# A two-sided adjacency product: half of the row groups turned in place by ScalarE and VectorE, in two rings of slots

## The chip, the cores and the metric

The kernel runs on one core of a Trainium2 chip. The metric is device time in microseconds (us), lower is better. Inputs and outputs are fp32.

## The reference

`x` is 5120 x 64 and `adj` is 5120 x 5120. Cut to what matters:

```
h = relu(layernorm(x))
e = par[0]*par[1] * (diag[:, None] * h @ W) + h      # users (rows 0:2048) and items have their own W, diag, par
h2 = adj @ (adj.T @ e)
out = x + layernorm(h2) * gamma + beta + h
```

The matrix `adj` (105 MB) is used twice: `adj.T @ e` sums over its rows, and the outer product sums over its columns, for which TensorE needs the tiles of `adj` transposed in SBUF.

## The kernel before

The columns of `adj` are cut into 5 panels of 1024, the rows into 10 groups of 512. One group of one panel is a slot: 128 partitions x 4 x 1024 fp32, 2 MB. Each panel has a **t phase**, in which `sum_t` adds the 10 groups' part of `adj.T @ e` into the PSUM bank `tT_ps`; a **finish**, in which `take_tT` copies the result out, TensorE turns it and `take_t` copies the turned blocks to `t_blocks` (a second set in another row order follows beside the first bank); and an **h phase**, in which `sum_h` adds this panel's part of `adj @ t` into 5 PSUM banks `h_ps`, one for each pair of groups, 8 column blocks of each. The last panel's h phase also has the output layernorm between its banks.

Before the h phase the tiles must be transposed. Three ways are in use, side by side:

- TensorE transposes 3 groups of each panel (4 in the first) in 128 x 128 tiles beside `sum_t` (L730, `turn_tiles`); ScalarE copies them back into the same slot (L430, `slot_back`).
- VectorE transposes 2 groups of each panel in 32 x 32 squares out of the slot into `at_ring`, 16 instructions of 32 x 512 for each half group (L569, `turn_units`); GpSimd copies them back into the slot (L345, `units_back`).
- The other 5 groups (4 in the first panel) are read from HBM a second time in an order in which 32 x 32 squares suffice (L252, `load_second`: two quadrants' DMAs on SP's queue and two on ScalarE's), and VectorE turns them block by block into `at_ring` during the h phase (L615, `turn_second`).

All 10 slots of a panel lie in SBUF (`panel`). The next panel's natural loads (L246, on SP's queue) follow in the order in which `sum_h` lets go of slots. The work is written out by hand for each engine, in order; panels 1 to 3 are a loop. In the first panel the "ego" chain (layernorm of `x`, relu, times W, `e_rows`) runs unit by unit beside the first groups of the t phase, on VectorE, ScalarE, TensorE and GpSimd in turn; TensorE's group 2k of the t phase needs unit k of `e`.

## Time and profile before

| what | value |
|---|---|
| median of 3 runs | 497.58 us (496.18 to 498.24) |
| profiled execution, its own time | 498.96 us |
| its span | 497.2 us |
| TensorE busy | 466.0 us, 94% |
| VectorE busy | 381.5 us, 77% |
| ScalarE busy | 101.0 us, 20% |
| GpSimd busy | 128.6 us, 26% |
| moved by DMA | 158.21 MB |

The span is the stretch of the records; the execution's own time is 1.8 us longer. A busy TensorE is not one at its peak, since the ends of matmuls are modelled; waits are therefore read from the chain of waits, whose pieces are listed in order of time with a start, a length and what ran. A releaser is the instruction whose semaphore ended a wait.

### The profile page before, as it was taken

The page shows a single profiled execution, that of the slowest core. Times are in us where ns is not written, and L with a number is a line of the kernel's source. Part 1 is how long each engine was busy: PE and PEld are TensorE (multiplying, and loading weights), DVE is VectorE, ACT ScalarE, POOL GpSimd, SP SyncE. Part 2 cuts the span into 40 slices and gives each one's busy share as a digit, 9 for nine tenths or more (in the row PEclk, how much of TensorE's full clock was granted, in tenths as well). Part 3 has the DMA queues.
Part 4 walks back from the last instruction along what each step waited for, and adds up shares of the span by engine and source line. Part 5 has one row for each costly group of instructions (what it writes and reads, how often), then busy time and mean ns, then how long its engine had stood idle before and what let it go on. Part 6 is the DMA issues. An engine that isn't in the chain of part 4 may idle for free.

```text
span 497.2 us, 6294 instructions
## 1 busy us (share of the span) xinstructions
PE 466.0 (94%) x2300; PEld 190.3 (38%) x2300; DVE 381.5 (77%) x523; ACT 101.0 (20%) x236; POOL 128.6 (26%) x111
## 2 busy tenths in 40 slices
PE   0799997999999899999999999999899999989996
PEld 0345543333443333244324324533433353344453
DVE  2768996868999735989984598999249899941793
ACT  2134442000340100025001002510200151022222
POOL 1121444180009500000852000075200005640223
PEclk9999999999999989999999999999899999979998
DMA  6999959999994999999599999969999996996001
GB/s 218 393 410 404 354 144 273 297 393 409 410 408 160 331 347 378 409 409 410 195 323 346 377 410 408 411 241 321 347 374 410 408 409 240 281 348 217 22 21 63
DMA packets 82114, 158.21 MB, mean 318 GB/s; under 512 B 4784, under 2 KB 56496, under 8 KB 82096
## 3 DMA queue, kind: packets, MB, share of 16 engines
q1 hardware_dynamic: 54864, 132.72, 72.3%
q10 hardware_dynamic: 27232, 25.26, 17.5%
q8 instruction: 11, 0.18, 0.1%
q14 instruction: 7, 0.06, 0.0%
HBM read 156.65 MB, written 1.31 MB: 318 GB/s over the span
## 4 chain that ended last, share of the span: by engine, by line
PE 69%; DVE 14%; issue 7%; ACTq 4%; DMA 2%; POOL 2%; ACT 1%; DVEq 0%; POOLq 0%
PE tT_ps L748 30%; PE h_ps L813 25%; PE tr_ps L730 10%; DVE at_ring L569 6%; DVE at_ring L615 6%; ACTq L252 3%; DMA diag_sb<-in_L_gnn_diag_i_dram 2%; POOL panel L345 2%; PE tr_ps L786 2%; PE tT_ps L759 1%; PE h_ps L716 1%; DVE e_sb L531 1%; DVE panel L529 0%; PE tT_ps L786 0%; ACT tT_quads L447 0%
## 5 line engine op out<-in xcount | busy, mean ns | idle before, releaser
L569 DVE STREAM_TRANSPOSE at_ring<-panel 32x512 f32<-32x512 f32 x320 | 224.8, 702 | 9.9 <-PE h_ps L813 5.3
L748 PE MATMUL tT_ps<-panel,e_sb 128*64 128x512 f32 x800 | 190.0, 607 | 2.9 <-DVE e_sb L531 2.9
L345 POOL TENSOR_TENSOR panel<-at_ring,ones_sb 128x512 f32<-128x512 f32 x80 | 103.0, 1326 | 288.7 <-PE tT_ps L748 227.7
L615 DVE STREAM_TRANSPOSE at_ring<-panel 128x1024 f32<-128x1024 f32 (+1 forms) x115 | 112.4, 1036 | 29.6 <-PE h_ps L813 21.5
L430 ACT ACTIVATE panel<-tr_ps 128x512 f32<-128x512 f32 x128 | 71.6, 595 | 231.1 <-PE tr_ps L730 230.7
L813 PE MATMUL h_ps<-panel,t_blocks 128*64 128x512 f32 x416 | 109.8, 616 | 0.5 <-POOL panel L345 0.5
L813 PE MATMUL h_ps<-at_ring,t_strided 128*64 128x512 f32 x384 | 100.9, 597 | 0.6
L748 PEld LDWEIGHTS tT_ps<-panel,e_sb 128*64 128x64 f32 x800 | 51.8, 138 | 91.2 <-issue 87.7
L730 PE MATMUL tr_ps<-ident,panel 128*128 128x128 f32 x512 | 76.5, 290 | 9.8 <-ACT tT_sb L446 5.1
L730 PEld LDWEIGHTS tr_ps<-ident,panel 128*128 128x128 f32 x512 | 57.2, 145 | 67.4 <-ACT panel L430 47.1
L813 PEld LDWEIGHTS h_ps<-panel,t_blocks 128*64 128x64 f32 x416 | 33.8, 143 | 67.6 <-issue 65.5
L813 PEld LDWEIGHTS h_ps<-at_ring,t_strided 128*64 128x64 f32 x384 | 30.0, 136 | 50.2 <-issue 28.0
L594 DVE COPY t_strided<-tT_ps 128x512 f32<-128x512 f32 x5 | 3.4, 685 | 26.4 <-PE tT_ps L759 26.4
L446 ACT ACTIVATE tT_sb<-tT_ps 64x512 f32<-64x512 f32 x5 | 3.0, 594 | 93.3 <-issue 51.7
L332 POOL TENSOR_TENSOR x_sb<-x_sb,e_sb 128x512 f32<-128x512 f32 x5 | 6.8, 1359 | 32.9 <-ACT e_sb L415 32.9
L377 POOL TENSOR_TENSOR panel<-panel,gamma_sb 128x512 f32<-128x512 f32 x4 | 5.1, 1273 | 39.3 <-DVE panel L646 39.3
L594 DVE COPY t_blocks<-tT_ps 128x512 f32<-128x512 f32 x5 | 3.5, 692 | 13.3 <-PE tT_ps L759 13.3
L708 PE MATMUL h_ps<-ident,e_sb 128*128 128x128 f32 x20 | 3.6, 309 | 9.9 <-ACT e_sb L415 9.9
L463 ACT ACTIVATE panel<-tr_ps 128x64 f32<-128x64 f32 x32 | 6.6, 239 | 20.3 <-PE tr_ps L786 20.3
L786 PEld LDWEIGHTS tr_ps<-c_blk,panel 128*128 128x128 f32 x36 | 8.8, 326 | 4.8 <-issue 3.2
L786 PE MATMUL tr_ps<-c_blk,panel 128*128 128x128 f32 x36 | 9.7, 411 | 0.7 <-ACT panel L478 0.7
L716 PE MATMUL h_ps<-w_blk,panel 128*128 128x128 f32 x40 | 6.6, 316 | 2.9 <-DMA w_blk<-in_L_gnn_W_i_dram 2.3
(57 smaller groups left out, 108.8 us busy)
## 6 DMA issues: line engine op xcount, KB each, us to landing
panel<-in_adj_dram SPq DMA_DIRECT2D x50, 2048.0 KB, 21.9
panel<-in_adj_dram SPq DMA_DIRECT2D x48, 512.0 KB, 11.5
panel<-in_adj_dram ACTq DMA_DIRECT2D x48, 512.0 KB, 12.7
x_sb<-in_x_dram SPq DMA_DIRECT2D x5, 256.0 KB, 8.7
out_dram<-x_sb SPq DMA_DIRECT2D x10, 128.0 KB, 1.8
w_blk<-in_L_gnn_W_u_dram SPq DMA_DIRECT2D x2, 16.0 KB, 10.1
w_blk<-in_L_gnn_W_i_dram SPq DMA_DIRECT2D x2, 16.0 KB, 9.2
gamma_sb<-in_L_gnn_ln_gamma_dram ACTq DMA_DIRECT2D x1, 32.0 KB, 6.6
```

Of the source, the lines that this page charges most:

```text
L252: eng.dma_start(dst, src.rearrange("(m p) c -> p m c", p=Q)).then_inc(second_in[g], 16)
L332: pool.tensor_tensor(unit(x_sb, u), unit(x_sb, u), unit(e_sb, u), ALU.add).then_inc(res_summed, 1)
L345: back = pool.tensor_tensor(dst, src, one, ALU.mult)
L430: nc.scalar.activation(dst, src, ACT.Copy).then_inc(tr_emptied, 1)
L569: turned = nc.vector.transpose(dst, src)
L594: nc.vector.tensor_copy(t[:, :, :], rows64(tT_ps[:, :])).then_inc(t_ready, 1)
L615: turned = nc.vector.transpose(at_ring[:, n % RING, halves, :].rearrange("p g (m c) -> p (g m) c", c=Q), slots_second(k, b, halves))
L716: last = nc.tensor.matmul(h_ps[u][:, j * P:(j + 1) * P], work(EGO_SLOT, 4 + u % 2)[:, j * P:(j + 1) * P], w_blk[:, 0 if u < USER_PAIRS els ...
L730: last = nc.tensor.transpose(tr_ps[n % 2][:, rb * P:(rb + 1) * P], slot_columns(g, b)[:, rb, :], ident[:, :])
L748: last = nc.tensor.matmul(tT_ps[half * D:(half + 1) * D, :], e_sb[:, g * RB + rb, :], slot_natural(g)[:, rb, half * BANK:(half + 1) * BANK ...
L786: last = nc.tensor.matmul(bank[:, rb * P:(rb + 1) * P], rows[:, rb, :], matrix[:, :], start=True, stop=True)
L813: last = nc.tensor.matmul(h_ps[k][half * D:(half + 1) * D, :], t[:, b, :], tile, start=False, stop=True, skip_group_check=True)
```

## The change

Each group now has a fixed kind. Groups 1, 3, 5, 7 and 9 are "move": ScalarE (9 squares of 32 partitions x 1024) and VectorE (the other 7) copy the group between partition quadrants from its natural slot into another slot, and VectorE then transposes that slot in place with two instructions of 128 x 2048. Groups 6 and 8 are "turn": TensorE transposes them as before, and ScalarE copies them out. Groups 0, 2 and 4 are "read": they are loaded a second time, straight into the other kind of slot, and VectorE turns them in place. GpSimd takes no part in this.

SBUF now holds two rings: `nat`, 4 natural slots, and `ready`, 8 slots of turned or second-read groups. A natural load waits until the load four places before it has been summed by TensorE and, by kind, moved by both engines or turned. A `ready` slot is free again when the bank eight places before has been summed. The order within a panel is 1, 3, 5, 7, 9, 6, 8, 0, 2, 4 from the second panel on (0 to 9 in the first), and the banks are the pairs (1,3), (5,7), (6,9), (0,8), (2,4). The panels are written out without a loop.

```diff
-    BY_PE = (4, 3, 3)
-    BY_DVE = (2, 2, 2)
+    KIND = ("read", "move", "read", "move", "read", "move", "turn", "move", "turn", "move")
+    BANKS = ((1, 3), (5, 7), (6, 9), (0, 8), (2, 4))
+    H_ORDER = (1, 3, 5, 7, 9, 6, 8, 0, 2, 4)
+    NATURAL = 4
+    TURNED = 8
+    ACT_MOVES = 9
...
-        panel = sb("panel", [P, GROUPS, RB * WIDTH])
+        nat = sb("nat", [P, NATURAL, SLOT])
+        ready = sb("ready", [P, TURNED, SLOT])
...
+        def wait_nat_free(eng, p, g):
+            n = loads_before(p, g) - NATURAL
+            if n >= 0:
+                p0, g0 = n // GROUPS, order(n // GROUPS)[n % GROUPS]
+                eng.wait_ge(t_summed, t_count(p0, g0))
+                if KIND[g0] == "move":
+                    eng.wait_ge(moved_act, move_count(p0, g0))
+                    eng.wait_ge(moved_dve, move_count(p0, g0))
+                if KIND[g0] == "turn":
+                    eng.wait_ge(tr_filled, tile_count(p0, g0) + BLOCKS)
+        def wait_ready_free(eng, p, g):
+            n = p * GROUPS + H_ORDER.index(g) - TURNED
+            if n >= 0:
+                eng.wait_ge(h_summed, h_count(n // GROUPS, H_ORDER[n % GROUPS]))
...
+        def move_blocks(p, g, blocks):
+            src, dst = nat_slot(p, g), ready_slot(p, g).rearrange("p (a r c) -> p a r c", a=NQ, r=RB)
+            for a, b in blocks:
+                yield (dst[b * Q:(b + 1) * Q, a, :, :], src[a * Q:(a + 1) * Q, :, b * SEG:(b + 1) * SEG])
...
+            for p in range(PANELS):                      # SP
+                second(p, READS[0])
+                if p < LAST:
+                    natural(p + 1, H_ORDER[0])
+                second(p, READS[1])
+                second(p, READS[2])
+                if p < LAST:
+                    for g in H_ORDER[1:]:
+                        natural(p + 1, g)
...
+            def move(p, g):                              # ScalarE; VectorE has the same with tensor_copy
+                act.wait_ge(natural_in[g], 16 * (p + 1))
+                wait_ready_free(act, p, g)
+                for dst, src in move_blocks(p, g, MOVE_BLOCKS[:ACT_MOVES]):
+                    last = nc.scalar.activation(dst, src, ACT.Copy)
+                last.then_inc(moved_act, 1)
...
                 egoT_copy(u)
+                if u == 1:
+                    move(0, MOVES[0])
+                if u == 3:
+                    move(0, MOVES[1])
...
+            def turn(p, g):                              # VectorE
+                if KIND[g] == "move":
+                    dve.wait_ge(moved_dve, move_count(p, g))
+                    dve.wait_ge(moved_act, move_count(p, g))
+                else:
+                    dve.wait_ge(second_in[g], 16 * NQ * (p + 1))
+                for half in range(2):
+                    part = ready_slot(p, g)[:, half * SLOT // 2:(half + 1) * SLOT // 2]
+                    last = nc.vector.transpose(part, part)
+                last.then_inc(turned, 1)
...
+                turn(p, READS[0])
+                move(p + 1, MOVES[0])
+                turn(p, READS[1])
+                turn(p, READS[2])
+                turn(p + 1, MOVES[0])
+                for g in MOVES[1:]:
+                    move(p + 1, g)
+                    turn(p + 1, g)
```

How instructions stand now is shown at three places. The first is ScalarE in the first panel, from the relu of ego unit 1 (`e_sb`) on; L407 and L363 copy the turned ego unit, L395 and L352 are its squares, L400 and L356 its root. Before:

```order
L415 ACTIVATE e_sb<-panel 128x512
L407 ACTIVATE panel<-h_ps 128x512
L395 ACTIVATE panel<-panel 128x512
L400 ACTIVATE stats<-stats,eps_sb 128x8
L415 ACTIVATE e_sb<-panel 128x512
L407 ACTIVATE panel<-h_ps 128x512
```

After, the same stretch and on to the last ego unit:

```order
L400 ACTIVATE e_sb<-ready 128x512
L363 ACTIVATE ready<-h_ps 128x512
L369 ACTIVATE ready<-nat 32x1024 x9
L352 ACTIVATE ready<-ready 128x512
L356 ACTIVATE stats<-stats,eps_sb 128x8
L400 ACTIVATE e_sb<-ready 128x512
L363 ACTIVATE ready<-h_ps 128x512
L352 ACTIVATE ready<-ready 128x512
L356 ACTIVATE stats<-stats,eps_sb 128x8
L400 ACTIVATE e_sb<-ready 128x512
L363 ACTIVATE ready<-h_ps 128x512
L369 ACTIVATE ready<-nat 32x1024 x9
```

Two blocks of nine copies now stand between ego units: behind unit 1 and behind unit 3.

The second place is VectorE in a middle panel, from the first copy of `tT_ps` on. Before, in the loop's body (L569 turns the next groups out of the slot, L615 the second reads):

```order
L569 STREAM_TRANSPOSE at_ring<-panel 32x16x32 x48
L559 ISA
L569 STREAM_TRANSPOSE at_ring<-panel 32x16x32 x16
L587 ISA
L588 COPY tT_sb<-tT_ps 64x512
L589 COPY tT_quads<-tT_ps 64x8x64
L593 ISA
L594 COPY t_blocks<-tT_ps 128x512
L631 REGISTER_ALU
L597 REGISTER_ALU
L615 STREAM_TRANSPOSE at_ring<-panel 128x512 x4
```

After (the second set of `t` is copied, one second read is turned, then the copies of the next panel's group 1, and so on):

```order
L554 COPY t_blocks<-tT_ps 128x512
L544 STREAM_TRANSPOSE ready<-ready 128x2048 x2
L533 COPY ready<-nat 32x1024 x7
L544 STREAM_TRANSPOSE ready<-ready 128x2048 x6
L533 COPY ready<-nat 32x1024 x7
L544 STREAM_TRANSPOSE ready<-ready 128x2048 x2
L533 COPY ready<-nat 32x1024 x7
L544 STREAM_TRANSPOSE ready<-ready 128x2048 x2
L533 COPY ready<-nat 32x1024 x7
L544 STREAM_TRANSPOSE ready<-ready 128x2048 x2
L533 COPY ready<-nat 32x1024 x7
L544 STREAM_TRANSPOSE ready<-ready 128x2048 x2
```

The 64 small transposes and the turning of second reads block by block have become five groups of 7 copies with whole-slot transposes between them.

The third place is SP's queue at the end of the first panel's natural loads. Before:

```order
L246 DMA panel<-in_adj_dram 128x4x1024 x8
L246 DMA panel<-in_adj_dram 128x4x1024 [waits e_ready]
L252 DMA panel<-in_adj_dram 32x16x256 [waits t_summed]
```

After:

```order
L233 DMA nat<-in_adj_dram 128x4x1024 x3
L233 DMA nat<-in_adj_dram 128x4x1024 [waits t_summed]
L233 DMA nat<-in_adj_dram 128x4x1024 [waits moved_dve,moved_act,t_summed]
L233 DMA nat<-in_adj_dram 128x4x1024 [waits t_summed]
L233 DMA nat<-in_adj_dram 128x4x1024 [waits moved_dve,moved_act,t_summed]
L233 DMA nat<-in_adj_dram 128x4x1024 [waits t_summed]
L233 DMA nat<-in_adj_dram 128x4x1024 [waits moved_dve,moved_act,t_summed]
```

Eight of the ten loads went out without a wait after the first; now six of them wait for TensorE, and three of these for both copying engines too.

## Rows read from the trace of the kernel before

**Rows 1.** The page: busy us (share of the span) x instructions, by engine.

```profile
PE 466.0 (94%) x2300; PEld 190.3 (38%) x2300; DVE 381.5 (77%) x523; ACT 101.0 (20%) x236; POOL 128.6 (26%) x111
```

**Rows 2.** The chain of waits in order of time: start us, us, what ran.

```profile
102.65 20.82 PE h_ps L813 x96
...
123.47 4.29 PE tT_ps L748 x20
127.77 1.03 PE tr_ps L730 x8
...
149.41 17.34 PE tT_ps L748 x80
166.90 0.85 ACTq L252
...
175.36 7.69 PE h_ps L813 x32
...
212.60 4.29 PE tT_ps L748 x20
...
389.82 4.29 PE tT_ps L748 x20
...
442.44 8.97 PE h_ps L813 x32
```

**Rows 3.** Groups by form: line, engine, out<-in, forms, count | busy us, mean ns.

```profile
L569 DVE STREAM_TRANSPOSE at_ring<-panel 32x512 f32<-32x512 f32 x320 | 224.8, 702 | 9.9 <-PE h_ps L813 5.3
L813 PE MATMUL h_ps<-panel,t_blocks 128*64 128x512 f32 x416 | 109.8, 616 | 0.5 <-POOL panel L345 0.5
L813 PE MATMUL h_ps<-at_ring,t_strided 128*64 128x512 f32 x384 | 100.9, 597 | 0.6
L615 DVE STREAM_TRANSPOSE at_ring<-panel 128x1024 f32<-128x1024 f32 x77 | 87.8, 1207 | 7.9 <-POOL panel L345 5.2 <-PE h_ps L813 2.2
L615 DVE STREAM_TRANSPOSE at_ring<-panel 128x512 f32<-128x512 f32 x38 | 24.6, 688 | 21.6 <-PE h_ps L813 19.3 <-POOL panel L345 1.6
L395 ACT ACTIVATE panel<-panel 128x512 f32<-128x512 f32 x5 | 3.1, 626 | 10.2 <-DVE panel L510 10.2
L478 ACT ACTIVATE panel<-h_ps 128x512 f32<-128x512 f32 x5 | 3.0, 599 | 14.4 <-PE h_ps L813 14.4
L488 ACT ACTIVATE panel<-tr_ps 128x256 f32<-128x256 f32 x1 | 0.4, 384 | 1.3 <-PE tr_ps L786 1.3
L547 DVE TENSOR_SCALAR diag_sb<-diag_sb,par_product 128x24 f32<-128x24 f32 x1 | 0.2, 238 | 0.0
L547 DVE TENSOR_SCALAR diag_sb<-diag_sb,par_product 128x16 f32<-128x16 f32 x1 | 0.2, 235 | 0.0
```

**Rows 4.** Instructions in order of time, finish of the first panel and after.

```profile
82.51 0.59 ACT L446 ACTIVATE tT_sb<-tT_ps 64x512 f32<-64x512 f32 x1 [9.13 <-issue]
83.01 0.58 ACT L447 ACTIVATE tT_quads<-tT_ps 64x512 f32<-64x512 f32 x1
83.69 0.63 PE L730 MATMUL tr_ps<-ident,panel 128*128 128x128 f32 x4 [3.34 <-ACT tT_sb L446]
87.01 7.53 PE L813 MATMUL h_ps<-panel,t_blocks 128*64 128x512 f32 x32
```

**Rows 5.** The same view, first panel, where the ego chain runs.

```profile
22.81 1.27 POOL L332 TENSOR_TENSOR x_sb<-x_sb,e_sb 128x512 f32<-128x512 f32 x1 [11.75 <-ACT e_sb L415]
23.56 0.55 DVE L509 TENSOR_SCALAR stats<-stats 128x8 f32<-128x8 f32 x1
24.88 0.60 ACT L407 ACTIVATE panel<-h_ps 128x512 f32<-128x512 f32 x1 [2.14 <-PE h_ps L708]
26.45 0.69 DVE L520 TENSOR_TENSOR panel<-panel,stats 128x512 f32<-128x512 f32 x1
29.63 0.17 DVE L509 TENSOR_SCALAR stats<-stats 128x8 f32<-128x8 f32 x1
```

**Rows 6.** DMA issues from 54 to 66 us: KB, us from issue to landing.

```profile
panel<-in_adj_dram SPq DMA_DIRECT2D x1, 2048.0 KB, 8.8
```

**Rows 7.** Stretches: us, busy us of PE, PEld, DVE, ACT, POOL; granted clock, DMA share, GB/s.

```profile
80.00:90.00 10.00, 6.66 (x36) 3.86 (x36) 5.77 (x9) 3.47 (x6) 4.73 (x4) 0.83 1.11 313
230.00:240.00 10.00, 10.00 (x54) 4.15 (x54) 9.79 (x15) 4.28 (x8) 1.87 (x2) 1.00 1.02 409
260.00:270.00 10.00, 8.71 (x50) 4.05 (x52) 3.80 (x7) 3.34 (x6) 3.87 (x4) 1.00 1.10 346
```

More of the change, by code:

```diff
@@ L393, in squares @@
                 act.wait_ge(centred, n + 1)
[L394 to L395 removed]
+                nc.scalar.activation(ego_work(2 + n % 2), ego_work(n % 2), ACT.Square).then_inc(squared, 1)
             def root(n):
@@ L451, in _ @@
-            panel_of_act(0)
-            with act.Fori(1, LAST) as p:
-                panel_of_act(p)
-            panel_of_act(LAST)
+            move(0, MOVES[2])
+            turn_back(0, 0)
+            turn_back(0, 1)
+            move(0, MOVES[3])
+            turn_back(0, 2)
+            turn_back(0, 3)
+            turn_back(0, 4)
+            second(0, READS[0])
+            turn_back(0, 5)
+            take_tT(0)
+            for batch in HELD:
+                turn_back(0, batch)
+            move(0, MOVES[4])
@@ new lines, in _ @@
+            for p in range(PANELS):
+                for g in READS[1:]:
+                    second(p, g)
+                if p < LAST:
+                    for g in MOVES:
+                        move(p + 1, g)
+                    for batch in range(HELD[0] - 1):
+                        turn_back(p + 1, batch)
+                    second(p + 1, READS[0])
+                    turn_back(p + 1, HELD[0] - 1)
+                    take_tT(p + 1)
+                    for batch in HELD:
+                        turn_back(p + 1, batch)
@@ L639, in _ @@
-            panel_of_dve(0)
-            with dve.Fori(1, LAST) as p:
-                panel_of_dve(p)
+                if u == 2:
+                    move(0, MOVES[0])
+            e_rows(PAIRS - 1)
+            turn(0, MOVES[0])
+            move(0, MOVES[1])
+            turn(0, MOVES[1])
+            for g in MOVES[2:4]:
+                move(0, g)
+                turn(0, g)
+            move(0, MOVES[4])
+            for p in range(PANELS):
+                take_tT(p)
+                take_t(p, 0, t_quads)
+                if p == 0:
+                    turn(0, MOVES[4])
+                take_t(p, 1, t_blocks)
+                if p == LAST:
+                    break
+                turn(p, READS[0])
[4 more added lines that the diff above has]
+                for g in MOVES[1:]:
+                    move(p + 1, g)
+                    turn(p + 1, g)
@@ L756, in turn_t, with sum_t @@
-            def turn_t(columns):
+            def sum_t(p, g):
+                at = order(p).index(g)
+                pe.wait_ge(natural_in[g], 16 * (p + 1))
+                if p and at == 0:
+                    pe.wait_ge(t_ready, 2 * p)
+                for r in range(RB):
+                    for half in range(2):
+                        last = nc.tensor.matmul(tT_ps[half * D:(half + 1) * D, :], e_sb[:, g * RB + r, :],
+                                                nat_slot(p, g)[:, r, half * BANK:(half + 1) * BANK],
+                                                start=(at == 0 and r == 0), stop=(at == GROUPS - 1 and r == RB - 1))
+                    if r == RB - 1:
+                        last.then_inc(t_summed, 1)
+                    if r % 2 == 1:
+                        batch = (BESIDE if p else BESIDE_FIRST).get((at, r // 2))
+                        if batch is not None:
+                            turn_tiles(p, batch)
@@ L826, in _ @@
             times_W(0)
-            for g in range(GROUPS):
+            for g in FIRST_ORDER:
                 if 1 <= g < PAIRS:
```

540 lines of the change are left out of this document (208 added, 332 removed).

## The prediction

> **What bounds the kernel now.** I read the busy shares first, then the chain of waits for the stage marks, then the groups by form for durations, and last the single instructions of the first panel. TensorE is busy 94% and VectorE 77%; ScalarE and GpSimd have room [rows 1]. The chain says what the 94% is made of [rows 2]: four transposed pairs of tiles (8 instructions, 1.03 us) stand between summing groups; five groups of the t phase take 17.34 us, so 3.47 us a group and 34.7 us for ten; three banks of the h phase take 20.82 us, so 6.94 us a bank and 34.7 us for five. A tile costs TensorE 0.51 us. A middle panel's work is 34.7 + 24 tiles x 0.51 (12.3) + 34.7 + about 1.2 for turning t = 82.9 us. The panels start at 123.5, 212.6 and 389.8 us, an average of 88.8 us. The other 6 us are waits, mostly at the finish, where ScalarE stands in its DMA issues ("ACTq" in the chain) before it can copy `tT_ps`. The h phases begin at 87.0 us [rows 4] (I call this mark H0), 175.4 (H1) and 442.4 (H4, last panel) [rows 2]; from H4 to the end of the span are 54.8 us. So before, TensorE is the bound, with a start of 87 us.
>
> **What the change takes away.** Tiles by TensorE: 8 of 24 in each of four panels and 16 of 32 in the first, together 48 x 0.51 = 24.5 us, all on the path. Second reads fall from 24 to 15 groups, 9 x 2.1 MB; DMA is not the bound of a whole panel, so I cost this at nothing. The finish loses ScalarE's issues in front of the copies: two DMAs instead of a handful stand there, and they are behind a tile copy, so I take 3.0 us from the last sum to the h phase (copy 1.4, turning t 0.55, copy 0.7, hand-overs). GpSimd's 103 us of copies go, but they ran beside TensorE and were waited for only in the first panel.
>
> **What it adds, in durations.** *ScalarE copy, 32 x 1024, SBUF to SBUF.* No row has it. 599 ns at 512 and 384 ns at 256 elements [rows 3] give 0.84 ns an element; 626 ns for SBUF to SBUF at 512 plus 512 x 0.84 is 1.05 us. Two in a row start 0.50 us apart though each lasts 0.59 [rows 4], so one follows the other about 0.10 sooner: 0.95 us, and 8.6 us for nine. Bounds: 0.85 (elements alone) and 1.05 (no overlap).
> *VectorE copy, 32 x 1024, SBUF to SBUF.* No row has it either. Upper bound: a transposition of 1024 elements, 1.21 us, 1.16 back to back. Lower bound: the two TENSOR_SCALAR rows, one source and all in SBUF as this is, differ by 3 ns for 8 elements, 0.4 ns each [rows 3]; 0.2 + 0.4 = 0.6 would be the whole copy. A second sign speaks for the faster end: the TENSOR_SCALAR at 23.56 us took 0.55 instead of 0.17 us and ended just as GpSimd's operation did (22.81 + 1.27 = 24.08) [rows 5], so such an operation takes a path to SBUF that GpSimd also uses. I take the end that these rows are nearest to, 0.63 us, 4.4 us for seven.
> The Trainium skill (VectorE: DVE Perf Modes, "The perf-mode tier table") says that an fp32 `tensor_copy` within SBUF runs at two elements a cycle, 1227 ns at 2048, and the skill's SBUF — State Buffer ("SBUF: two separate sides") says that such an operation shares a port pair with GpSimd under a lock; the trace's row at 23.56 us agrees. From the page's figure I estimate 0.69 us a copy, 4.8 us for seven; the sum below would end some 10 us later by it.
> *VectorE transposition in place, 128 x 2048.* 1207 - 688 = 519 ns for 512 more elements [rows 3], so 1.16 + 1.04 = 2.20 us, 4.4 us a group. A copied group thus costs VectorE 8.8 us, a second read 4.4. A panel has 5 x 8.8 + 3 x 4.4 + 2.8 = 60 us of VectorE work against 76 before: fine as a share, so what matters is order.
> *A natural load with nothing ahead of it.* 8.8 us from issue to landing [rows 6]; in a stream one lands every 5.1 us (2.1 MB at 409 GB/s), second reads run at 346 [rows 7]. Before, ten slots keep this latency out of sight; four slots do not.
> *Strided reading by TensorE* (128-byte pieces in the h phase): pieces of 512 bytes took 616 ns and contiguous tiles 597 [rows 3]; I cost it at nothing, at most 3% of 210 us.
>
> **A middle panel, with H = 0 at the start of its h phase.** Banks end at 7.0, 14.5 (turning t is between), 21.5, 28.4 and 35.4. VectorE: second set of t and first read by 12.7; then the copies of the next panel's group 1 wait for bank 1's slot, 14.5 to 18.9; two reads and group 1 are turned, 32.1 (bank 4 needs the reads by 28.4: 27.7, just in time); then copies 3, turn, copies 5, turn, copies 7, turn, copies 9: 4 x 4.4 + 3 x 4.4 = 30.8, done 62.9. Only then may the load four places on (group 2) be issued; it lands at 71.7. TensorE, free of waits, wants it at 35.4 + 8 x 3.47 + 4 pairs of tiles x 1.02 = 67.3: it waits 4.4 us. The group takes 3.5 + 2.0, the last group 3.5: 80.7. Finish 3.0: 83.7. ScalarE runs beside this: group 3 lands at about 28 (7.0 + 12.1 for second reads + 5.1 + 3.5 of latency), four times 8.6 from there is 62.4, just ahead of VectorE. A wait of 3.34 us before was followed by a clock of 0.83 over ten us [rows 4, 7], 1.2 GHz for part of it, some 1.7 us lost; I add half of that: 84.5 us a panel, 4.3 less than before. Tiles alone would have given 4.1 and the finish 4; the new wait takes half of that back.
>
> **The first panel.** ScalarE's copies of group 1 start when its ego copy at 24.9 is done [rows 5]: 25.5 to 34.1. Behind them on ScalarE stands the root of unit 2, for which VectorE's norm waits (at 26.45 before), then relu, TensorE's turning, `e_rows`. TensorE's third group starts at 37.6. VectorE's copies (4.4) stand before unit 4's centring, and ScalarE's second block, 47.6 to 56.2, before unit 4's root; the last `e_rows` ends at 66.8. Only now VectorE turns group 1 (71.2) and copies its part of group 3 (75.6), which frees the slot for group 7: it lands at 84.4, while TensorE has been idle since 72.2. Group 7 with its tiles and a slow clock: 91.6. ScalarE copies group 7 from 91.9 to 100.5, and TensorE's fourth pair of tiles and VectorE's turn of group 7 wait for it; VectorE turns (104.9), copies group 9 (109.3) and only then copies `tT_ps`: H0 = 112.0, 25 later than 87.0.
> ScalarE then copies group 9 (120.9) and issues its half of two second reads; VectorE turns 9, 0, copies (1,1), turns 2 and 4: 143.6; bank 4 until 150.6; copies of (1,9) done at 178.8, load 187.6, two groups 196.6, finish 199.6, slow clock 1.7: H1 = 201.3 against 175.4.
> **Sum.** H4 = 201.3 + 3 x 84.5 = 454.8. From H4 on the same work stands, the first bank without waits: 54.0. Span 508.8, against 497.2: +11.6. The profiled execution's own time was 498.96, its median neighbours 497.58, 1.4 less; so 498.96 + 11.6 - 1.4 = 509 us. In terms: tiles and finish -8 a panel over four panels and the slot waits +4 (-17), start +25, second panel's late turning +3 and small change.
> About 155 VectorE copies lie on this path, so 0.05 us on one moves the sum by 8; with 0.6 to 0.7 the likeliest case spans 500 to 524.
>
> **Rivals.**
> *TensorE stays the bound (faster).* If VectorE's copies take 0.5 us or less, or a lone load lands 4.4 us sooner (the stream's 5.1 speaks for something shorter, the row's 8.8 against), or both in part, the ninth group is there by 67.3 and a panel takes 35.4 + 34.7 + 6.1 + 3.0 = about 79.5. H1 = 193, H4 = 431.6, span 485.6: 486 us. The point from which it decides is the copies of group 9 being done 4.4 us earlier.
> *ScalarE frees the slots last.* Without the overlap, 1.05 us a copy, four groups from 28 end at 65.8, 2.9 after VectorE: 12 us over four panels and 3 in the first: 523 us. For it: ScalarE's rows on 32 partitions across quadrants don't exist. Against: the starts 0.50 apart.
> *VectorE's copies at one element a cycle,* 1.16 us: 3.7 more a group, 18.5 a panel, and 11 in the first: H1 = 231, H4 = 540, 594 us. For it: every other VectorE slope in the rows. Against: the two signs above.
>
> **How the numbers follow.** Likeliest case 0.55, TensorE-bound 0.22, ScalarE last 0.13, slow copies 0.07, anything else 0.03. Within 0.5% is about what a measurement can tell from no change (495.1 to 500.1). Faster: 0.22 and 0.03 of the likeliest; same: 0.10 from its lower edge; slower: the rest, 0.65. The range 485 to 526 just takes in the first rival and the ScalarE one, and leaves out the slow copies and what is worse than the ends of these three.
>
> **What would show it.** The likeliest case wants: VectorE COPY at 0.6 to 0.7 us; TensorE waiting 3 to 5 us for the ninth natural load of each later panel; h phases starting near 112 and 201 us and then every 84 to 85; DMA idle for some 20 us in the first panel. It is wrong if H0 comes before 100 or after 120, or if a middle panel takes under 81 or over 88 us.

## The result and the profile after

The changed kernel takes 541.7 us (median of 4 runs, 538.86 to 544.46), the one before 497.62 (496.18 to 498.24): a ratio of 1.089, 95% interval 1.0829 to 1.0951. It is slower by 9%; the forecast was 509 us and a range of 485 to 526. The profiled execution took 538.86 us with a span of 537.0, the fastest of the four; spans below are compared with the forecast's 508.8 and the 497.2 of before.

| start of | before | forecast | after |
|---|---|---|---|
| first h phase (H0) | 87.0 | 112.0 | 118.8 |
| second (H1) | 175.3 | 201.3 | 212.2 |
| third | 263.5 | | 306.1 |
| fourth | 352.2 | | 395.0 |
| fifth (H4) | 442.4 | 454.8 | 489.5 |
| end of the span | 497.2 | 508.8 | 537.0 |

The page of the changed kernel, busy us (share) x instructions and the granted clock in 40 slices:

```profile
span 537.0 us, 5378 instructions
PE 445.0 (83%) x2108; PEld 179.7 (33%) x2108; DVE 343.5 (64%) x338; ACT 312.5 (58%) x415; POOL 26.9 (5%) x30
PEclk9968795899979999999989899998999999799999
```

TensorE is busy 21 us less than in [rows 1] (fewer tiles, but also slower matmuls, as shown below), and the span is 40 us longer: it waits 61 us more. The lowest clock (0.5) is in the seventh slice, 80.6 to 94.0 us, in the first panel, and it is 0.6 to 0.8 in four others of the first eight.

The groups by form (line, engine, operation, tiles and forms, count | busy us, mean ns | idle just before, and who ended it). L673 sums in the t phase and L731 in the h phase, L369 and L533 are the copies of the "move" groups on ScalarE and VectorE, and L544 turns a slot:

```profile
L369 ACT ACTIVATE ready<-nat 32x1024 f32<-32x1024 f32 x225 | 237.4, 1055 | 65.2 <-PE h_ps L731 47.0 <-DMA nat<-in_adj_dram 15.4 <-issue 0.3
L673 PE MATMUL tT_ps<-nat,e_sb 128*64 128x512 f32 x800 | 199.6, 646 | 31.8 <-DMA nat<-in_adj_dram 28.9 <-DVE e_sb L521 2.9
L544 DVE STREAM_TRANSPOSE ready<-ready 128x2048 f32<-128x2048 f32 x80 | 179.5, 2287 | 24.4 <-ACT ready L369 18.2 <-DMA ready<-in_adj_dram 5.5
L731 PE MATMUL h_ps<-ready,t_quads 128*64 128x512 f32 x640 | 178.4, 604 | 7.9 <-DVE ready L544 7.9
L533 DVE COPY ready<-nat 32x1024 f32<-32x1024 f32 x175 | 121.1, 692 | 8.7 <-PE h_ps L731 6.0
```

The three prices that no row of before had are the mean ns of the first, third and fifth line: 1055 for a ScalarE copy (forecast 950, bounds 850 to 1050), 2287 for an in-place transposition (2200), 692 for a VectorE copy (630). The summing in the t phase (L673) waits 28.9 us for natural loads and is busy 199.6 us at 646 ns; the same 800 matmuls of before (L748) were busy 190.0 us at 607 ns with no wait for a load.

One middle panel, TensorE in order of time (start us, us, ..., idle before and releaser); its h phase began at 306.1. L662 are pairs of tiles, and L379 on ScalarE copies them out (below: its turn-backs):

```profile
365.05 2.76 PE L673 MATMUL tT_ps<-nat,e_sb 128*64 128x512 f32 x8 [2.09 <-DMA nat<-in_adj_dram]
367.74 1.90 PE L662 MATMUL tr_ps<-ident,nat 128*128 128x128 f32 x8
369.57 1.94 PE L673 MATMUL tT_ps<-nat,e_sb 128*64 128x512 f32 x8
372.82 1.15 PE L662 MATMUL tr_ps<-ident,nat 128*128 128x128 f32 x8 [1.31 <-ACT ready L379]
...
380.71 1.94 PE L673 MATMUL tT_ps<-nat,e_sb 128*64 128x512 f32 x8 [0.95 <-DMA nat<-in_adj_dram]
...
388.20 3.65 PE L673 MATMUL tT_ps<-nat,e_sb 128*64 128x512 f32 x16 [1.64 <-DMA nat<-in_adj_dram]
```

Four waits stand here where the forecast had one of 4.4 us for the ninth group (the one at 380.71, and it is 0.95; in the other later panels the ninth group waits 2.58 us or not at all). The seventh group waits for its load; the second pair of tiles waits for ScalarE, whose turn-back of the first pair is queued behind all its copies; the tenth group waits for its load. The pair at 367.74 takes 1.90 us instead of 1.1: a slower clock behind the first wait.

The two copying engines in the same panel end nearly together, ScalarE's 66.0 us after the start of the h phase (372.14) and VectorE's 66.7 (372.81); the forecast had 62.4 and 62.9. ScalarE first, then VectorE:

```profile
333.70 38.44 ACT L369 ACTIVATE ready<-nat 32x1024 f32<-32x1024 f32 x36 [3.16 <-DMA nat<-in_adj_dram]
372.17 1.09 ACT L379 ACTIVATE ready<-tr_ps 128x512 f32<-128x512 f32 x2
```
```profile
363.39 4.50 DVE L544 STREAM_TRANSPOSE ready<-ready 128x2048 f32<-128x2048 f32 x2
367.92 4.89 DVE L533 COPY ready<-nat 32x1024 f32<-32x1024 f32 x7
```

36 ScalarE copies in 38.44 us are 1.07 us each: they do not overlap at all. Where ScalarE is later still against TensorE, in the panel before, the wait for it is 4.44 us, and the matmuls behind the load wait are slow:

```profile
279.65 1.97 PE L662 MATMUL tr_ps<-ident,nat 128*128 128x128 f32 x8 [4.44 <-ACT ready L379]
281.55 3.18 PE L673 MATMUL tT_ps<-nat,e_sb 128*64 128x512 f32 x8
...
297.58 5.35 PE L673 MATMUL tT_ps<-nat,e_sb 128*64 128x512 f32 x16 [3.15 <-DMA nat<-in_adj_dram]
```

16 matmuls took 5.35 us here and 3.65 in the other panel. That panel took 94.0 us, the other 88.9, and the next one 94.5 (waits for ScalarE 4.44, 1.31 and 3.12 us).

The first panel, TensorE around its longest waits, and then bank 4 (the last, counted from 0), which waits in its h phase:

```profile
87.28 3.68 PE L673 MATMUL tT_ps<-nat,e_sb 128*64 128x512 f32 x8 [12.15 <-DMA nat<-in_adj_dram]
90.89 1.97 PE L662 MATMUL tr_ps<-ident,nat 128*128 128x128 f32 x8
...
106.63 1.97 PE L662 MATMUL tr_ps<-ident,nat 128*128 128x128 f32 x8 [6.06 <-ACT ready L379]
...
118.78 7.09 PE L731 MATMUL h_ps<-ready,t_quads 128*64 128x512 f32 x32
```
```profile
152.54 9.69 PE L731 MATMUL h_ps<-ready,t_quads 128*64 128x512 f32 x32 [4.34 <-DVE ready L544]
```

The stretch around the load wait (start and end, us, busy of PE, PEld, DVE, ACT, POOL, granted clock, DMA share, GB/s):

```profile
79.00:93.00 14.00, 5.72 (x18) 2.56 (x20) 13.82 (x12) 0.70 (x2) 0.00 (x0) 0.51 0.87 335
342.00:350.00 8.00, 8.00 (x40) 3.22 (x38) 7.88 (x8) 7.89 (x9) 0.00 (x0) 1.00 0.50 177
```

The granted clock is 0.51 in the first, which is the level of 1.2 GHz, and 1.00 (2.4 GHz) in the second, where TensorE had summed without a pause. The eight matmuls at 87.28 took 3.68 us against 1.94 at full clock.

### The profile page after: what moved, and what is told of

It is laid out like the page before. It is cut to its first block, busy times and chain, and to the rows that moved or that the text cites. A ratio compares the mean times of both kernels' runs of the same rounds, so it can differ in the third digit from the quotient of the medians.

```text
span 537.0 us, 5378 instructions
## 1 busy us (share of the span) xinstructions
PE 445.0 (83%) x2108; PEld 179.7 (33%) x2108; DVE 343.5 (64%) x338; ACT 312.5 (58%) x415; POOL 26.9 (5%) x30
## 3 DMA queue, kind: packets, MB, share of 16 engines
HBM read 137.78 MB, written 1.31 MB: 259 GB/s over the span
## 4 chain that ended last, share of the span: by engine, by line
PE 29%; ACT 22%; DMA 22%; DVE 18%; issue 6%; ACTq 1%; SPq 1%; DVEq 0%
ACT ready L369 20%; DMA nat<-in_adj_dram 17%; PE tT_ps L673 11%; PE h_ps L731 10%; DVE ready L544 8%; DVE ready L533 7%; PE tr_ps L662 5%; DMA ready<-in_adj_dram 3%; DMA diag_sb<-in_L_gnn_diag_i_dram 2%; ACT ready L379 1%; PE tr_ps L710 1%; PE tT_ps L686 1%; ACTq L239 1%; SPq L239 1%; DVE tT_sb L550 1%
## 5 line engine op out<-in xcount | busy, mean ns | idle before, releaser
L369 ACT ACTIVATE ready<-nat 32x1024 f32<-32x1024 f32 x225 | 237.4, 1055 | 65.2 <-PE h_ps L731 47.0
L673 PE MATMUL tT_ps<-nat,e_sb 128*64 128x512 f32 x800 | 199.6, 646 | 31.8 <-DMA nat<-in_adj_dram 28.9
L544 DVE STREAM_TRANSPOSE ready<-ready 128x2048 f32<-128x2048 f32 x80 | 179.5, 2287 | 24.4 <-ACT ready L369 18.2
L731 PE MATMUL h_ps<-ready,t_quads 128*64 128x512 f32 x640 | 178.4, 604 | 7.9 <-DVE ready L544 7.9
L533 DVE COPY ready<-nat 32x1024 f32<-32x1024 f32 x175 | 121.1, 692 | 8.7 <-PE h_ps L731 6.0
L673 PEld LDWEIGHTS tT_ps<-nat,e_sb 128*64 128x64 f32 x800 | 62.1, 147 | 141.4 <-issue 101.8
L731 PEld LDWEIGHTS h_ps<-ready,t_quads 128*64 128x64 f32 x640 | 56.9, 139 | 94.5 <-issue 93.2
L379 ACT ACTIVATE ready<-tr_ps 128x512 f32<-128x512 f32 x80 | 44.0, 595 | 71.9 <-PE tr_ps L662 71.7
L731 PE MATMUL h_ps<-ready,t_blocks 128*64 128x512 f32 x160 | 70.0, 593 | 0.7 <-DVE t_blocks L554 0.7
L662 PE MATMUL tr_ps<-ident,nat 128*128 128x128 f32 x320 | 49.0, 302 | 15.2 <-ACT ready L379 15.2
L662 PEld LDWEIGHTS tr_ps<-ident,nat 128*128 128x128 f32 x320 | 38.6, 154 | 47.4 <-issue 27.9
L731 PEld LDWEIGHTS h_ps<-ready,t_blocks 128*64 128x64 f32 x160 | 21.7, 137 | 23.0 <-issue 21.3
L352 ACT ACTIVATE ready<-ready 128x512 f32<-128x512 f32 x5 | 3.2, 631 | 16.2 <-DVE ready L501 16.1
(54 smaller groups left out, 118.8 us busy)
## 6 DMA issues: line engine op xcount, KB each, us to landing
ready<-in_L_gnn_W_u_dram SPq DMA_DIRECT2D x2, 16.0 KB, 10.1
```

The source lines that it names most:

```text
L369: last = nc.scalar.activation(dst, src, ACT.Copy)
L379: nc.scalar.activation(ready_slot(p, g)[:, b * BANK:(b + 1) * BANK], tr_ps[n % 2][:, :], ACT.Copy).then_inc(tr_emptied, 1)
L533: last = nc.vector.tensor_copy(dst, src)
L544: last = nc.vector.transpose(part, part)
L662: last = nc.tensor.transpose(tr_ps[n % 2][:, r * P:(r + 1) * P], nat_slot(p, g)[:, r, b * P:(b + 1) * P], ident[:, :])
L673: last = nc.tensor.matmul(tT_ps[half * D:(half + 1) * D, :], e_sb[:, g * RB + r, :], nat_slot(p, g)[:, r, half * BANK:(half + 1) * BANK], ...
```

## The experiments

All ratios are to the kernel before, with its runs on the same chip (medians 496.4 to 497.9). "A panel" is the mean distance of h phases from the second to the fifth: 92.4 in the changed kernel (93.4 from the first to the second), 89.0 before. My theory after reading the two traces: the start costs 32 us because copies stand between ego units, and a middle panel is set by the copying engines freeing four natural slots. The rivals: the loads alone bound a panel, ScalarE alone does, or VectorE alone.

One caution on the first panel, whose ego chain is the same in eight traces (but for the number of squares that each engine copies): H0 stands at 118.7 to 120.2 in seven of them and at 113.7 in the eighth (`tiles_early`). For one, the 16 matmuls in front of the last ego unit took 5.89 us in `copies_first7` and 3.65 in `tiles_early`, though no edit separates the two there:

```profile
59.77 5.89 PE L673 MATMUL tT_ps<-nat,e_sb 128*64 128x512 f32 x16
```
```profile
58.79 3.65 PE L673 MATMUL tT_ps<-nat,e_sb 128*64 128x512 f32 x16
```

The runs of these two kernels fall in pairs with the same distance: 520.8, 520.9, 525.3 and 526.0 us, and 505.1, 505.2, 510.0 and 510.1. What makes the matmuls of a run slow there no run shows. So 5 us of a total can come from there without any edit; lengths of panels and single rows are the safer reading.

**Copies behind the ego chain** (`ego_first`). 521.33 us, 1.0426 (1.0333 to 1.052).

```diff
-                if u == 1:
-                    move(0, MOVES[0])
-                if u == 3:
-                    move(0, MOVES[1])
...
+            move(0, MOVES[0])
+            move(0, MOVES[1])
             move(0, MOVES[2])
```

(VectorE likewise: its copies of group 1 stand behind the last unit's norm.)

> First panel: ScalarE's and VectorE's copies of groups 1 and 3 come behind the ego chain instead of inside it. Theory A (the copies stand in the ego chain and so hold back every later release of the first panel): last e_rows near 48 us instead of 68, ScalarE's copies of groups 1, 3, 5 run 41.7 to 70.5, the first h phase starts near 96 us instead of 118.8, total about 519. Rival B (the four natural slots alone cost the start, wherever the copies stand): first h phase still after 112 us, total 531 or more.

The first h phase starts at 100.1 instead of 118.8 (96 expected), and a panel keeps its length, 92.6. So of the 31.8 us that the start lost, 18.7 by these two traces (13.6 against the earliest start above) are the copies between ego units. What waits now is the load of group 5, which leaves at 52.2, when ScalarE's first nine copies are done, and then ScalarE's turn-backs:

```profile
60.01 9.64 PE L670 MATMUL tT_ps<-nat,e_sb 128*64 128x512 f32 x32 [13.70 <-DMA nat<-in_adj_dram]
86.92 1.97 PE L659 MATMUL tr_ps<-ident,nat 128*128 128x128 f32 x8 [6.06 <-ACT ready L379]
```

**A natural load ahead of the second reads** (`load3_early`). 539.76 us, 1.086 (1.0807 to 1.0913).

```diff
                     natural(p + 1, H_ORDER[0])
+                    natural(p + 1, H_ORDER[1])
                 second(p, READS[1])
```

> Only SP's order differs: the natural load of the next panel's group 3 is issued before the second reads of groups 2 and 4, so it does not wait for bank 0. Theory A (in a middle panel ScalarE frees the slots last: group 3 lands 28.4 us into the h phase, then four groups at 9.6 us end at 66.8, VectorE's at 66.4): ScalarE is some 4 us sooner, the load of group 2 then goes by VectorE, a panel loses a little TensorE waiting at the tiles too: 88 to 89 us a panel instead of 92.4, total about 524. Rival B (VectorE's chain alone sets the release): no change, 537.

Nothing came of it: a panel is 92.3 us, not 88 to 89. ScalarE can start group 3 sooner, but the second reads land later and VectorE turns them before it copies group 3. Its last copies end at 375.5 with the h phase at 306.3, 2.5 us later against it than in the changed kernel. Over the three middle panels it both gives and takes: TensorE's tiles no longer wait for ScalarE at all (8.9 us in the changed kernel), but the banks of the h phase wait 12.4 us for VectorE instead of 3.5, and the loads are waited for as before.

**Half of each copy's elements** (`act_half`, `dve_half`, `both_half`; one run each). From the second panel on the copies move 512 of 1024 elements, on ScalarE, on VectorE or on both; the rest of each square isn't written.

```diff
+                few = RB // 2 if p else RB
                 for dst, src in move_blocks(p, g, MOVE_BLOCKS[:ACT_MOVES]):
-                    last = nc.scalar.activation(dst, src, ACT.Copy)
+                    last = nc.scalar.activation(dst[:, 0:few, :], src[:, 0:few, :], ACT.Copy)
```

> From the second panel on ScalarE's copies move only half of each square (32 x 512 instead of 32 x 1024); what is left out keeps old data. First panel as in the changed kernel. Theory A (ScalarE frees the slots last and keeps TensorE's tiles of group 6 waiting): ScalarE ends near 54 us of the h phase, VectorE's 66.4 decides, a panel takes 87 to 88 us instead of 92.4, total about 518. Rival B (VectorE alone decides): 92 us a panel, 537.

> From the second panel on VectorE's copies move only half of each square; what is left out keeps old data. Theory A (ScalarE frees the slots last): VectorE ends near 57 us of the h phase, ScalarE still at 66.8, a panel stays at 92 us, total 535 to 537. Rival B (VectorE alone decides): its chain is 9 us shorter, a panel takes 84 us, total about 505.

> From the second panel on ScalarE's and VectorE's copies both move only half of each square; what is left out keeps old data. First panel as in the changed kernel. Theory C (both copying chains end together, near 66.5 us of the h phase, so that halving one leaves the other; behind them stand the stream of six loads in the t phase and the load of group 4, whose slot waits for the tiles of group 6): both end before 58, TensorE still waits some 2 us for the stream and 3 us for group 4, a panel takes 85 to 87 us instead of 92.4, total about 512. Rival D (the copies are all that holds the panel): TensorE is the bound again, 80 us a panel, total about 488. Rival E (the ring's loads are all, the copies nothing): 89 us or more, 528 or more.

| | time | span | a panel |
|---|---|---|---|
| after | 541.7 | 537.0 | 92.4 |
| VectorE's halved | 535.42 | 533.6 | 92.7 |
| ScalarE's halved | 530.88 | 529.1 | 89.0 |
| both halved | 523.05 | 521.2 | 88.0 |

ScalarE's copies fell to 628 ns each, and a panel by 3.4 us. That is a mean: the two panels of 94.0 and 94.5 us lose 4.7 and 5.3, the one of 88.9 loses 0.3, so what ScalarE costs is mostly its late turn-backs. VectorE's alone gave a panel nothing; its span is shorter by 3.4 us because H0 to H1 fell from 93.4 to 89.4: bank 4's wait for VectorE is 2.48 us there instead of 4.34, and no slow matmuls follow the ninth group's load in the t phase behind it. With both halved 4.4 us of a panel are won (I had expected 5 to 7), and 8.5 us above the 79.5 of TensorE's own work (the forecast's first rival) stay. So far as halving shows it, copies are thus the smaller part of what holds up a middle panel. The trace with ScalarE's halved shows what is next:

```profile
378.15 3.28 PE L674 MATMUL tT_ps<-nat,e_sb 128*64 128x512 f32 x8 [3.52 <-DMA nat<-in_adj_dram]
```

There the ninth group waits 3.5 us for its load, behind VectorE's copies of group 9. This is the step as it was forecast, and it shows at that size only once ScalarE is out of its way.

**All copies of a middle panel ahead of the transpositions of the copied groups, 7 squares for ScalarE and 9 for VectorE** (`copies_first7`). 523.1 us, 1.0527 (1.0461 to 1.0593).

```diff
-    ACT_MOVES = 9
+    ACT_MOVES = 7
...
-                turn(p + 1, MOVES[0])
                 for g in MOVES[1:]:
                     move(p + 1, g)
+                for g in MOVES:
                     turn(p + 1, g)
```

> Output as the reference. In the middle panels VectorE makes all its copies before it turns the copied groups, and the split of squares is 7 for ScalarE and 9 for VectorE. First panel's order unchanged, its split is 7 to 9 too. Theory C: slots are released near 58 us of the h phase instead of 66.5 and ScalarE no longer keeps the tiles of group 6 waiting; a panel takes about 86 us, total 508 to 518. Rival E (ring's loads alone): 92, 537.

A panel is 88.7 us (86 expected), within 0.7 of the kernel with both engines' copies halved: the copies hardly count any more. What is left is in two rows:

```profile
358.24 1.94 PE L673 MATMUL tT_ps<-nat,e_sb 128*64 128x512 f32 x8 [2.09 <-DMA nat<-in_adj_dram]
...
378.56 5.22 PE L673 MATMUL tT_ps<-nat,e_sb 128*64 128x512 f32 x16 [2.89 <-DMA nat<-in_adj_dram]
```

The first is the seventh group. The fifth load of a t phase can only be issued once its first group is summed; in the panel shown above that is at 345.8, and it lands at 353.6. The sixth lands at 358.7 and the seventh at 365.0, 5.1 and 6.3 us behind one another, and TensorE wants the seventh at 342.16 + 6 x 3.47 = 363.0. This wait is in both kernels to the hundredth, 2.09: VectorE's copies of group 5 hold the issue of the seventh load for 1.4 us in the changed kernel and not at all here, and it lands 22.8 us into the t phase in both. The second is the tenth group: its load waits for the slot of group 6, whose eighth tile is turned only behind the eighth group. In the changed kernel this load leaves at 379.8 and lands at 388.2, while TensorE has half of group 2 twice and two pairs of tiles to do, 5.8 us: the wait is set by where the tiles stand, whatever the copies take.

**The three together** (`all_three`; in the first panel it also puts ScalarE's copies of group 7 ahead of its first turn-backs, and VectorE's copies ahead of more of its turns). 520.78 us, 1.0455 (1.0388 to 1.0522).

> Output as the reference. The ego chain free of copies, VectorE's copies before its turns with a 7 to 9 split, group 3's load before the second reads. If the costs of the first panel and of the middle panels are separate, they add: first h phase near 96 us, then about 86 us a panel and 47.5 for the end, total 488 to 496, so at or below the kernel before. If the one only hides the other: 505 or more.

H0 came at 98.2, but a panel rose to 93.7 us. That is 5.0 more than in `copies_first7`, and the early natural load is the likely cause, though no run has it on `copies_first7` alone: VectorE's turns of second reads waited 11.3 us in all for their DMAs (3.1 in `copies_first7`), and banks of the h phase 17.9 us for VectorE (8.1):

```profile
L730 PE MATMUL h_ps<-ready,t_quads 128*64 128x512 f32 x640 | 184.6, 625 | 17.9 <-DVE ready L543 17.9
L543 DVE STREAM_TRANSPOSE ready<-ready 128x2048 f32<-128x2048 f32 x80 | 178.0, 2281 | 16.6 <-DMA ready<-in_adj_dram 11.3 <-ACT ready L370 5.0
```

In `load3_early` it took from the banks what it gave to the tiles; with the split of 7 to 9 no tile waits for ScalarE any more in a middle panel, and only the cost is left. I had expected 488 to 496 us.

**Tiles half a group sooner** (`tiles_early`, on `copies_first7`). 507.6 us, 1.0221 (1.0173 to 1.027).

```diff
-    BESIDE = {(6, 0): 0, (6, 1): 1, (7, 0): 2, (7, 1): 3, (8, 0): 4, (8, 1): 5}
+    BESIDE = {(5, 1): 0, (6, 0): 1, (6, 1): 2, (7, 0): 3, (7, 1): 4, (8, 0): 5}
```

> Output as the reference. On top of copies_first7 (copies before turns, split 7 to 9): from the second panel on TensorE's pairs of tiles stand half a group sooner, so that group 6 is all turned in the middle of the eighth group and not at its end, and its slot goes to the load of group 4 some 3 us sooner. Theory C (the last wait of a panel is group 4's load behind the tiles of group 6, 2.9 us, and the slow clock behind it, 1.6 us): both go, 84 to 85 us a panel instead of 88.7, total 503 to 509. Rival H (the stream of six loads would hold the last group anyway): 88 us a panel, 520 to 524.

**Natural loads of half the columns** (`half_loads`, on `copies_first7`; one run, 502.73 us). From the second panel on each natural load brings 512 of the 1024 columns; all else is as it was, on stale data.

```diff
-            eng.dma_start(nat_slot(p, g), src.rearrange("(p r) c -> p r c", p=P)).then_inc(natural_in[g], 16)
+            few = WIDTH // 2 if p else WIDTH
+            eng.dma_start(nat_slot(p, g)[:, :, 0:few], src.rearrange("(p r) c -> p r c", p=P)[:, :, 0:few]).then_inc(natural_in[g], 16)
```

> copies_first7 with natural loads that from the second panel on bring only the first half of the columns; the rest of a slot keeps old data. Theory C (behind the copies it is the loads into four slots that hold a panel): the stream and group 4 are no longer waited for, 81 to 83 us a panel, total 494 to 502. Rival (TensorE and VectorE alone make the 88.7): 88 us or more, 520 to 524.

`tiles_early` gave 84.4 us a panel, `half_loads` 82.5. TensorE's waits in one middle panel (what waited, for what: us in total, times, longest), first of `copies_first7`, then of `tiles_early`:

```profile
PE tT_ps L673 <- DMA nat<-in_adj_dram: 5.0, 2, 2.9
PE h_ps L731 <- DVE ready L544: 1.7, 1, 1.7
PE tT_ps L686 <- DVE tT_sb L550: 0.5, 1, 0.5
```
```profile
PE tT_ps L673 <- DMA nat<-in_adj_dram: 2.2, 2, 1.2
```

(The other two are as above in both.) With tiles sooner the tenth group's load leaves some 2 us earlier against TensorE, and the pair of tiles moved ahead fills part of the seventh group's wait. The waits for loads fall by 2.8 us, and behind the tenth no half clock follows:

```profile
364.21 3.65 PE L673 MATMUL tT_ps<-nat,e_sb 128*64 128x512 f32 x16 [0.91 <-DMA nat<-in_adj_dram]
```

16 matmuls take 3.65 us, where `copies_first7` had 5.22: 1.6 more, together about the 4.3 us of a panel. The granted clock of this whole panel is 1.00. With half of each load no wait for one above 0.2 us is left in two of the three middle panels (one of 1.7 stands in the other), which confirms that these waits are the loads'.

**The output's columns in the order that TensorE reads** (`before_hT`, one part of the change alone, on the kernel before). 492.23 us over 12 runs, 0.9905 (0.9871 to 0.994).

```diff
-                nc.scalar.activation(work(OUT_SLOT, 4 + k % 2), h_ps[k][:, :], ACT.Copy).then_inc(hT_ready, 1)
+                nc.scalar.activation(work(OUT_SLOT, 4 + k % 2).rearrange("d (r p) -> d p r", r=RB),
+                                     h_ps[k][:, :].rearrange("d (p r) -> d p r", r=RB), ACT.Copy).then_inc(hT_ready, 1)
...
-                rows = work(OUT_SLOT, 4 + k % 2).rearrange("d (p r) -> d r p", r=RB)
+                rows = work(OUT_SLOT, 4 + k % 2).rearrange("d (r p) -> d r p", r=RB)
```

> The kernel before with one part of the change alone: ScalarE writes the copy of h_ps in the order in which TensorE reads it, so TensorE's weights in the output layernorm are contiguous instead of every fourth element. Theory F (the end of the changed kernel is 7 us shorter because of these strided weights: 8 instructions of a bank took 2.07 us before and 1.09 after): four banks between h banks save 1.0 us each and the last one about 2, total 491 to 493. Rival G (the shorter end is from what stood on the engines before the last panel, not from the weights): no change, 497.5.

From H4 to the end it is 48.2 us against 54.8 before and 47.5 after, so this accounts for 6.6 of the 7.3 us. TensorE's weights are `rows`; in the kernel before their elements lay 16 bytes apart, here they are contiguous. The rows of before, of this kernel, and the copy of the changed one:

```profile
L786 PE MATMUL tr_ps<-c_blk,panel 128*128 128x128 f32 x36 | 9.7, 411 | 0.7 <-ACT panel L478 0.7
L786 PEld LDWEIGHTS tr_ps<-c_blk,panel 128*128 128x128 f32 x36 | 8.8, 326 | 4.8 <-issue 3.2 <-ACT panel L478 1.6
```
```profile
L787 PE MATMUL tr_ps<-c_blk,panel 128*128 128x128 f32 x36 | 5.3, 289 | 1.2 <-ACT panel L478 1.2
L787 PEld LDWEIGHTS tr_ps<-c_blk,panel 128*128 128x128 f32 x36 | 4.4, 191 | 5.3 <-issue 3.2 <-ACT panel L478 2.0
L478 ACT ACTIVATE panel<-h_ps 128x512 f32<-128x512 f32 x5 | 5.4, 1079 | 12.7 <-PE h_ps L814 12.7
```
```profile
L465 ACT ACTIVATE nat<-h_ps 128x512 f32<-128x512 f32 x3 | 1.8, 597 | 11.9 <-issue 8.8 <-PE h_ps L731 3.1
```

ScalarE pays 1079 instead of 599 ns for its copy [rows 3], five times, because here it writes with a stride; the changed kernel writes in plain order and permutes what it reads from PSUM, and pays 597.

**What the parts give together** (`ego_copies_tiles`: the order of copies, the ego chain and the tiles, without the early load). 488.02 us, 0.9814 (0.9788 to 0.984).

> Output as the reference. The ego chain free of copies, the copies before the turns with the 7 to 9 split, and the tiles half a group sooner; the order of loads as in the changed kernel. If the costs add: first h phase at 98 us, then 88 and three times 84 to 85, end 47.5: total 484 to 492, below the kernel before. If they hide each other: 500 or more.

H0 is 97.2, and a panel 84.3 us. The gains add up, then, once the early load is left out. In its first panel nine VectorE copies took 11.15 us, beside GpSimd adding `beta`:

```profile
41.87 11.15 DVE L531 COPY ready<-nat 32x1024 f32<-32x1024 f32 x9
```
```profile
44.17 8.28 POOL L315 TENSOR_TENSOR x_sb<-x_sb,beta_sb 128x512 f32<-128x512 f32 x5 [3.55 <-DMA beta_sb<-in_L_gnn_ln_beta_dram]
```

**GpSimd's additions moved behind the last t phase** (`beta_late`, on the one above). 485.23 us, 0.9778 (0.974 to 0.9815).

> Output as the reference. ego_copies_tiles with GpSimd's five additions of beta moved from the first panel behind the last t phase. Theory K (a VectorE copy within SBUF and a GpSimd operation exclude each other: nine copies took 11.15 us beside these additions and 6.3 elsewhere): the first nine copies take about 6.5 us, the slot of group 1 comes free by ScalarE near 50 us instead of 53, the first h phase starts 1 to 3 us sooner, total 484 to 487. Rival L (the copies are slow there for another reason, such as the DMA stream at full rate): the nine still take 11 us, total 488.

```profile
42.50 6.29 DVE L530 COPY ready<-nat 32x1024 f32<-32x1024 f32 x9
```
```profile
434.87 6.20 POOL L328 TENSOR_TENSOR x_sb<-x_sb,beta_sb 128x512 f32<-128x512 f32 x5
```

Beside each other the nine copies took 4.9 us longer and the five additions 2.1; H0 moves from 97.2 to 94.1. This is the fastest kernel, 2.2% under the one before and 10.4% under the changed one: the same division of the groups, in another order.

## Why the prediction was wrong

The sign was right and so was the place of the loss at the start, but the time lay above the range. Against the forecast span of 508.8 the measured one is 28.2 longer: H0 +6.8, H0 to H1 +4.1, the three middle panels +23.8, the end -6.5. Of the 4.5 us more between the medians (541.7 less 509), 2.8 are that the profiled execution was the fastest of its four, 1.4 that the forecast had allowed for one that was slower than its neighbours, and the rest is rounding. The forecast's own sign of being wrong, a middle panel of over 88 us, came; H0 stayed just under its 120.

- **Durations.** The step "Two in a row start 0.50 us apart though each lasts 0.59, so one follows the other about 0.10 sooner: 0.95 us" failed: these copies start 1.067 apart, 9.6 us for nine and not 8.6. VectorE's seven took 4.89, not 4.4, a group's transpositions 4.50, not 4.4. The 0.63 us a copy behind the 4.4 came from two single rows 3 ns apart, and that so small a difference pointed to the right end was luck. The estimate of 4.8 from the Trainium skill (VectorE: DVE Perf Modes, "The perf-mode tier table"), which stood outside the sum, was the better value, and the trace agrees with it: 0.69 us a copy. That puts the engines' last copies at 66.0 and 66.7 instead of 62.4 and 62.9. The case of ScalarE freeing slots last had the right 1.05 us and still too small a price, 3 us a panel, since it counted only the slots: behind ScalarE's copies also stand its turn-backs, for which TensorE's tiles wait (4.44, 1.31 and 3.12 us in the three middle panels). Halving ScalarE's copies alone gave 3.4 us a panel, VectorE's nothing: so ScalarE, and not VectorE as forecast, set the pace of two of the three panels, by its turn-backs and not by the slots.
- **A middle panel, "TensorE, free of waits, wants it at 67.3".** This is the step that failed most. TensorE is not free of waits before the ninth group, nor behind it: in the panel shown it comes to the ninth group 73.7 us after the start of the h phase and not 67.3. The forecast followed one chain (copies of group 9, slot, ninth load) and never asked of the seventh and tenth load what releases them. `copies_first7` and `both_half` show a panel 8.5 to 9.2 us above TensorE's 79.5 with the copies out of the way, and `tiles_early` and `half_loads` took 4.3 and 6.2 of these away. Of the rest in `tiles_early`, 4.9 us, 3.9 are the waits for loads (2.2) and for VectorE in the h phase (1.7); the last 1.0 is that 79.5 was short: TensorE is busy 79.9 us there and waits 0.5 in the finish. (The prediction's own terms, 35.4, 34.7, 6.1 and 3.0, give 79.2.) In the changed kernel's three middle panels the waits are 10.1, 7.2 and 9.8 us: for loads 4.0, 4.7 and 4.6, for ScalarE's turn-backs 4.4, 1.3 and 3.1, for VectorE 1.2, 0.7 and 1.6, and 0.5 each in the finish.
- **The clock.** Half of 1.7 us was added once a panel. In the rows above every wait of 2.89 us or more has matmuls at the slow rate behind it, and of the two of 2.09 us one has (365.05) and one hasn't (358.24). TensorE is busy 83.8, 81.7 and 84.7 us in the three middle panels and 79.9 in one at full clock (`tiles_early`): 3.5 us a panel on average where the forecast had 0.85. (L673's 800 matmuls are busy 9.6 us more than L748's, but 5.5 of these are in the first panel.) So of the 7.9 us by which a middle panel is longer than forecast, 2.6 are the clock and 5.3 the waits.
- **The first panel.** The chain through ScalarE's copies between ego units, VectorE and the lone load was right step by step, as was the DMA queues' idle stretch of some 20 us (no load between 57.2 and 79.6): the first block at 24.5, the second at 48.5 to 58.1 (forecast 47.6 to 56.2), the load at 79.6 to 87.3 (forecast 75.6 to 84.4), TensorE's fourth pair of tiles waiting for ScalarE. Of the 6.8 us by which H0 is late, the durations above are 4.2; 3.0 are matmuls that the slow clock made longer than forecast, in front of the last ego unit (1.4) and behind the wait for the load (1.6); 0.6 is the finish, and the load itself was 1.1 shorter. `ego_first` shows that the place of the copies is 18.7 us of the loss, or 13.6. In H1's part the forecast had bank 4 start at 143.6, 31.6 after H0 and with a wait of 3.2 us; it started 33.8 after H0 with a wait of 4.34 (152.54), and its matmuls took 9.5 us until the t phase and not 7.0: +2.2 and +2.5, less 0.6 in the t phase, is the +4.1.
- **The end** was costed as "the same work", 54.0. It was 47.5: the change in the layout of `rows` was in the diff of the kernel and not costed at all. `before_hT` shows it alone.
- **Right:** the finish (3.0 forecast, about 3.2 from the last sum to the h phase in a middle panel: 391.8 to 395.0), the removed tiles and second reads, strided reading at nothing (594 ns against 592 for contiguous, at full clock, below), the slow-copy case out, the load's 8.8 us (7.7 to 8.8).

"Faster" was possible with this division, but not in this order. That the case of TensorE as the bound had 486 us and `ego_copies_tiles` and `beta_late` reach 488 and 485 is chance: they have panels of 84.3 and a start of 94 to 97 instead of 79.5 and 112.

## What to carry to other kernels

When buffers get few, write down for every load which instruction frees its slot, and when; the one chain that looks longest is not the sum of the waits, and here waits for two loads that no faster copy brings forward cost as much as the engines' copies. Long copies queued on an engine that also hands back small results delay those results: put the small ones first, or move them. In these traces a wait of TensorE of some 3 us cost about half as much again, because matmuls behind it ran at the slow clock (2.89 us of wait, then 5.22 us for what takes 3.65).

## What the runs showed of the hardware

- ScalarE's copies of 32 x 1024 from SBUF to SBUF take 1055 ns, of 32 x 512 628 ns, and start 1067 ns apart without any overlap; two copies of 128 x 512 from PSUM (595 ns each) take 1.09 us and do overlap. The Trainium skill (ScalarE: Activation LUTs, "What ACT_TABLE_LOAD costs") gives 186 ns + 0.833 ns an element, by which I estimate 1039 and 612, and the trace agrees; it also says that ACTIVATEs back to back overlap by some 93 ns, and the trace agrees for the copies from PSUM and doesn't for these.
- VectorE's fp32 copies in SBUF and GpSimd's additions hold each other up: nine copies took 11.15 us beside them and 6.29 alone, five additions 8.28 and 6.20. One behind another they would take 12.5 us. The Trainium skill (SBUF — State Buffer, "SBUF: two separate sides") tells of a port pair that the two share under a lock, and the measurement agrees: only some 1.3 us of the two overlapped.
- fp32 weights whose elements lie 16 bytes apart load in 326 ns instead of 191, and the matmul that follows takes 411 instead of 289. The moving operand in pieces of 128 bytes (`t_quads`) costs nothing against a contiguous one (`t_blocks`): the means over the whole trace, 604 and 593 ns, differ because more of the former stand behind waits, at the slow clock. From 212 to 248 us, at a granted clock of 1.00:

```profile
L731 PE MATMUL h_ps<-ready,t_quads 128*64 128x512 f32 x126 | 34.6, 594 | 1.2 <-DVE ready L544 1.2
L731 PE MATMUL h_ps<-ready,t_blocks 128*64 128x512 f32 x32 | 13.9, 592 | 0.0
```

- A 128 x 512 fp32 copy by ScalarE from PSUM takes 599 ns in plain order, 597 when it reads in another order (runs of 32 elements or every fourth) and writes plainly, and 1079 when it writes with a stride of 128 elements.
